# First attention of a four-layer kernel: three hand-written issue orders changed on TensorE, ScalarE and VectorE

## What is computed

```
ln_out = _ln(hidden_states, ln_w, ln_b)
q  = _ln(_fp8_linear_pertensor(ln_out, wq, ...))      # 16 heads of 128
k  = _ln(_fp8_linear_pertensor(ln_out, wk, ...))      # 8 groups, two heads share one
v  =     _fp8_linear_pertensor(ln_out, wv, ...)
core = _gqa(q, k, v)                                  # softmax(q k / sqrt(128)) v
qx = _ln(_fp8_linear_pertensor(ln_out, wqx, ...))
kx, vx = split(einsum(cond, w_kv_x)); kx = _ln(kx)
xout = _gqa(qx, kx, vx)
catq = _div_clamp_fp8(concatenate([core, xout]), proj_smooth)
out  = einsum(catq, wproj) * (proj_in_scale * proj_w_scale)
```

## Time and profile before

| what | value |
|---|---|
| median of 3 runs | 1542.64 us (1542.45 to 1543.8) |
| span of the profiled execution, first to last instruction | 1540.9 us |
| mean granted TensorE clock of the core | 0.985 |
| busy shares over the span | PE 94%, DVE 58%, ACT 49%, POOL 34% |
| the first attention in the trace | about 22 to 470 us |
| query copies (L753) / key copies (L758) | 64 / 32 |
| mean of one query copy, one key copy | 797 ns, 780 ns |

### The profile page before, as it was taken

One profiled execution on the slowest core, in us unless ns is written; L12 is line 12 of the kernel. 1 busy time (PEld: TensorE's weight loads), 2 busy tenths in 40 slices (PEclk: granted clock), 3 DMA queues, 4 the chain that ended last, 5 costly groups with the idle time before them and its releaser, 6 DMA issues. The chain is left out here.

```text
span 1540.9 us, 22220 instructions
## 1 busy us (share of the span) xinstructions
PE 1443.8 (94%) x6908; PEld 1036.8 (67%) x6910; DVE 895.8 (58%) x1940; ACT 762.5 (49%) x2116; POOL 528.4 (34%) x519
## 2 busy tenths in 40 slices
PE   4999998899999999999999999999968999999998
PEld 1677777777874555557787979776745666665656
DVE  7888988888875242323555454554686555553322
ACT  4888888888882211110343535343456555544210
POOL 2667677877761000000542424221111333321000
PEclk9999999999999999999999999999979999999999
DMA  5211000200007311112100000002141000001120
GB/s 198 80 41 59 8 5 1 94 1 1 1 1 291 144 57 48 54 49 76 66 1 1 1 0 9 20 1 83 37 181 45 1 1 1 1 29 34 51 64 21
DMA packets 21304, 71.65 MB, mean 47 GB/s; under 512 B 3859, under 2 KB 6291, under 8 KB 18245
## 3 DMA queue, kind: packets, MB, share of 16 engines
q1 hardware_dynamic: 12980, 57.37, 10.0%
q10 hardware_dynamic: 8208, 12.87, 2.6%
HBM read 69.01 MB, written 1.22 MB: 46 GB/s over the span
## 5 line engine op out<-in xcount | busy, mean ns | idle before, releaser
L1190 ACT ACTIVATE l0f_silu<-bank 128x512 f32<-128x512 f32 x48 | 28.6, 597 | 199.9 <-PE bank L1114 189.8
L828 POOL TENSOR_TENSOR l0a_stepped<-l0a_y,l0a_m 128x512 f32<-128x512 bf16 x64 | 74.0, 1156 | 94.4 <-DVE l0a_m L575 93.0
L1293 DVE TENSOR_TENSOR l0f_product<-l0f_silu,bank 128x512 f32<-128x512 f32 x48 | 32.9, 688 | 123.8 <-ACT l0f_silu L1190 123.7
L856 POOL TENSOR_TENSOR l0a_head_rstd<-l0a_head_var,all_minus_half 128x4 f32<-128x4 f32 x96 | 100.8, 1054 | 7.6 <-DVE l0a_head_var L597 7.6
L427 PEld LDWEIGHTS bank<-l0a_k_t,l0a_q_t 128*128 128x128 f32 x512 | 63.2, 191 | 49.1 <-ACT l0a_q_t L753 45.1
L767 ACT ACTIVATE l0a_work<-bank,l0a_neg_max 128x128 f32<-128x128 f32 x256 | 90.2, 370 | 0.9 <-DVE l0a_neg_max L610 0.9
L1126 PEld LDWEIGHTS bank<-all_weights_a,l0f_hidden 128*128 128x128 f32 x384 | 72.9, 190 | 25.2 <-issue 17.0
L1730 DVE TENSOR_TENSOR all_weights_a<-bank,all_cols 128x512 f32<-128x512 f32 x64 | 43.9, 690 | 77.9 <-PE bank L1559 45.9
L1126 PE MATMUL bank<-all_weights_a,l0f_hidden 128*128 128x256 f32 x384 | 88.9, 379 | 0.0
L427 PE MATMUL bank<-l0a_k_t,l0a_q_t 128*128 128x128 f32 x512 | 72.1, 284 | 17.1 <-ACT l0a_q_t L753 16.7
L2608 POOL TENSOR_TENSOR l3a_q_scale<-l3a_q_var,all_minus_half 128x4 f32<-128x4 f32 x32 | 32.4, 1013 | 159.7 <-DVE l3a_q_var L2398 159.7
(11 more groups left out here) (434 smaller groups left out, 3825.8 us busy)
## 6 DMA issues: line engine op xcount, KB each, us to landing
l0f_spread<-l0f_weights ACTq DMA_DIRECT2D x32, 192.0 KB, 2.7
all_weights_a<-in_l_w_q SPq DMA_DIRECT2D x2, 2048.0 KB, 14.5
l0f_spread<-l0f_weights ACTq DMA_DIRECT2D x32, 128.0 KB, 2.9
all_weights_b<-in_l_e_gate_up SPq DMA_DIRECT2D x1, 3200.0 KB, 10.6
all_weights_b<-in_l_e_gate SPq DMA_DIRECT2D x1, 3072.0 KB, 10.2
all_weights_a<-in_l_e_up SPq DMA_DIRECT2D x4, 768.0 KB, 7.2
all_weights_a<-in_l_e_down SPq DMA_DIRECT2D x1, 3072.0 KB, 16.8
l3a_spread<-l3f_weights SPq DMA_DIRECT2D x10, 256.0 KB, 3.5
```

The source lines that it names most:

```text
L828: done = g.tensor_tensor(stepped[:, 0:n], value, step, ALU.add)
L856: g.tensor_tensor(head_rstd[:, m % 2, :], head_var[:, m % 2, :], res.minus_half[:, 0:HU], ALU.pow)\
```

## The change

Three lists of `march` in `layer0_attention` are reordered. No instruction is added, removed or altered, and no wait is.

```
 PE:
-                               in_tile(F_TILE, first_up, F_UP), (project_out, later(at_query, 11)),
-                               (turn, later(at_norm, 3)), (project, range(STEPS))])
+                               in_tile(F_TILE, first_up, F_UP), (turn, later(at_norm, 3)),
+                               (project_out, later(at_query, 11)), (project, range(STEPS))])
 DVE:
-            march(VTS, STEPS, [(variance, later(at_norm, 1)), (row_inverse, later(at_query, 5)),
-                               (row_max, later(at_query, 4)), (normalise, later(at_norm, 2)),
+            march(VTS, STEPS, [(variance, later(at_norm, 1)), (row_max, later(at_query, 4)),
+                               (normalise, later(at_norm, 2)), (row_inverse, later(at_query, 5)),
 ACT:
-            march(VTS, STEPS, [(exponentials, later(at_query, 5)), (scale_probs, later(at_query, 6)),
-
-                               (keep_values, later(at_plain, 1)), (keep_turned, later(at_norm, 3)),
+            march(VTS, STEPS, [(keep_turned, later(at_norm, 3)), (exponentials, later(at_query, 5)),
+                               (scale_probs, later(at_query, 6)), (keep_values, later(at_plain, 1)),
                                (prepare, range(STEPS)), (keep_probs, later(at_query, 7)), (square, at_norm),
```

## The result

The changed kernel takes 1590.53 us (median of 4 runs, 1587.45 to 1592.28) against 1542.55 us before in the same runs. The ratio is 1.0309, 95% interval 1.0295 to 1.0323: slower by 3.1%, some 48 us. Forecast were 1592 us, in a range of 1573 to 1611.

What follows compares the result with a forecast made beforehand. PE was taken to bound the cross half outright and to share the bound in the core half. Terms 40 + 6 + 4 = 50 us on a span of 1540.9, plus 1.7, gave about 1592 us, range 1573 to 1611.

Steps and rivals of the forecast that it cites:

- The deciding term: Odd steps: key copies ahead of scaling on ACT delay PE's turn_probs by 1.28 us, 31 times, 40 us.
- up to 6 us may come back: Tiles 8 and 9: a longer tile lets late DVE and POOL catch up, returning up to 6 us.
- The even steps: Query copy ahead of exponentials: scores need both, starting 2.19 to 2.22 us after the copy, so order wins nothing.
- the late copy of step 6: Core tiles, step 6: the query copy comes 0.31 us later than the exponentials started before.
- The ring in core tiles: Steps 6 and 0: copy, exponentials, DVE, turn take 6.52 us against 6.29; two pairs in 8 tiles, 4 us.
- The six places at 1.0 us: Tiles 4 to 7: PE's earlier turn waits for normalised rows where DVE has extra work, 6 us.
- DVE's list: Steps 2 and 4: normalise fills the time until the later exponentials end, costed at nothing.
- the PE waits: Rival: PE's 16.7 us of waits before the scores disappear, giving 1526 us; chance 4%.
- a draw: Rival: even steps tie and key scaling is somehow covered, giving 1543 us; chance 3%.
- only queries move: Rival: lists do not bring key copies ahead of scaling, so 6 + 4 remain, 1553 us; chance 5%.
- a bound by DVE: Rival: slow rounding closes the ring or late normalising pushes the next, 1612 us or above; chance 8%.
- cross tiles of 28.6 us: Sign of being right: a cross tile lasts some 28.6 us in place of 26.

Runs made afterwards that it cites:

- e1: Changed kernel with key copies back behind scale_probs and keep_values on ACT, query copies still ahead of the exponentials: 1557.20 us, ratio 1.0098.
- e2: Kernel before with key copies alone moved ahead of scale_probs on ACT: 1574.40 us, ratio 1.0207.
- e9: Changed kernel with PE turning keys right behind the scores, ahead of mix, ACT's list untouched: 1567.91 us, ratio 1.0163.
- e3: Kernel before with PE's list alone as in the change, turn ahead of project_out: 1543.46 us, ratio 1.0009.
- e5: Kernel of e1 with quantise, quantise_early and centre_queries put ahead of row_inverse on DVE: 1553.92 us, ratio 1.0073.
- e6: Changed kernel with DVE's old list, reciprocals ahead of row maximum and normalising: 1591.63 us, ratio 1.0320.
- e7: Kernel before with DVE's new list alone, row maximum and normalising ahead of reciprocals: 1542.98 us, ratio 1.0001.

## Why the prediction was right, and where its terms were not

**The deciding term.** Key copies ahead of `scale_probs` were predicted to hold `turn_probs` by 1.28 us, 31 times, 40 us. The mechanism is shown by e1, e2 and e9. The hold measured is 1.25 to 1.27 us in each place, and the size in all is 33.3 us (e1 against the changed kernel). The count was one too high: the first scaling starts at 50.22 us, behind the key copies of both step 3 and step 5 of tile 0 (34.26 and 43.61), so 30 holds are left. In cross tiles 1 to 7 the difference of the two kernels is 2.54 us a tile, where two times 1.28 is 2.56. In core tiles 10 to 13 it is 2.40. The term was too large at its edges: tile 8 gives 0.1 back, tile 9 takes 1.4, and tiles 0 and 15, with one hold each, take 0.0 and 1.2. The prediction had put "up to 6 us may come back" in tiles 8 and 9 into the lower end, not into the sum; 3.8 came back there.

**The even steps.** The score needs copy and exponentials, whatever their order: right. Where PE waits before scores in the changed kernel, in 38 places, exponentials end the wait, never the query copy, and e1 gained nothing. Only three of the 38 lie before 259 us: in nearly all of the cross half PE comes to the scores too late to wait. But the sum is not equal. From copy to scores it takes 2.32 us and not 2.19 to 2.22; the row below the reciprocal shows PE starting 1.64 after the first exponential (373.57 to 375.21), where DVE starts 1.52 after it. This 0.1 us comes four times a tile. Together with the late copy of step 6 (0.31, as predicted) it makes the 0.67 us by which e1's core tiles are longer (26.12 against 25.45): the four pairs are longer by 0.44, 0.08, 0.08 and 0.07.

**The ring in core tiles.** "Copy, exponentials, DVE 3.64, turn: 6.52" was the wrong reason, and that the term came out near its size is luck: 4 us stood in the sum, and in e1 core tiles 10 to 13 are 2.7 us longer by the release and the late copy just told, and tile 14 is 2.1 longer for a reason not settled. The pair of steps 6 and 0 takes 6.35 after the change. From the reciprocal to the end of `normalise` it is 2.57 us now (375.09 to 377.66), not 3.64, and PE does not wait for the rows (`turn_probs` 377.96, turn 0.44 later). I had carried over a stretch that held a slow rounding instruction.

**The six places at 1.0 us.** This step failed in its reasoning: e3 has the earlier turn and loses 0.8 us, within noise. A DVE that is late by a constant is waited for once. It is waited for again and again only when its lateness comes round: in the company of ACT's new order the reciprocal depends on exponentials that depend on the turned query. e1 is 1.01 us a tile longer than before in tiles 1 to 7, 7.1 in all, of which the slower release, four times 0.08 a tile, is 2.2 us at most; e5 takes about 3 us out of the ring. In the changed kernel PE does wait for rows in tiles 5 to 7, twice in each, 0.41 to 1.68 us, where about 1 us was named; but it also waits in tiles 2 to 4, for 3.6 us in five places, where the prediction had the rows in time. Parts of the 7.1 us, and 2.1 us in tile 14 of e1, are not settled.

**DVE's list.** Costed at nothing; e6 and e7 agree.

**The sum.** 40 + 6 + 4 stood against 33.3 + 14.6. Errors of 7 too much and 5 too little met in a total that is 2 off; that it is so close is luck. The rivals: the PE waits did not go, they rose from 16.7 to 24.3 us; a draw, "only queries move" as a reading of the code, and a bound by DVE did not come about. The time that "only queries move" was given, 1553, was measured in e1 as 1557. The page Perfetto Trace Analysis of the Trainium skill (section Optimization Strategy) asks for what a gap waits on to start sooner; e3 did this for the turn and e1 for the copy, and neither shortened the time (1543.46 and 1557.20 us against 1542.67): in e3 the copy still stood behind the exponentials on ACT, and in e1 the scores waited for the exponentials, now behind the copy.

**What was named as a sign:** 50 us of waits before key copies (54.9 came), some 30 waits before `turn_probs` of over 1 us (30, longest 1.1), cross tiles of 28.6 us (30.35 came, of which the kernel before already had 26.80 and not 26), core tiles of 28.3 (28.52), a cross window with PE under 37 of 40 us (35.32).

## What to carry to other kernels

When a list of work is reordered for one kind of item, look at every kind that the same entry handles, and at what then waits in front of it: here the queries were meant and the keys cost two thirds of the loss. Moving one of two conditions of a wait forward gains nothing when the other takes its place on the same in-order engine. A late producer costs its lateness once; it costs it each time only if its start depends on the consumer, so look for the ring before multiplying.

## What the runs showed of the hardware

A rounding instruction of 256 elements on DVE takes 0.23 us or over 1 us, by what POOL does. In the kernel before, steps 6 and 7 of tile 12:

```profile
365.81 1.16 POOL L832 TENSOR_TENSOR l0a_cat<-l0a_stepped,l0a_m 128x512 fp32r<-128x512 f32 x1 [0.16 <-issue]
365.83 1.22 DVE L571 TENSOR_SCALAR l0a_e<-l0a_yq 128x256 uint16<-128x256 uint16 x1
```

It starts 0.02 after a POOL product of 1.16 us and ends with it. In the changed kernel the same instruction of the same step, here of tile 11, meets an idle POOL, whose next product comes 0.7 later:

```profile
375.67 0.23 DVE L571 TENSOR_SCALAR l0a_e<-l0a_yq 128x256 uint16<-128x256 uint16 x1
...
376.37 0.67 POOL L827 TENSOR_TENSOR l0a_stepped<-l0a_yq,l0a_mq 128x256 f32<-128x256 bf16 x1 [1.28 <-DVE l0a_mq L575]
```

It takes 0.23 us. The Trainium skill, page SBUF — State Buffer, section Who interferes with whom, says that a DVE `tensor_scalar` may use a second pair of ports which it shares with GpSimd, and that whoever comes second waits for the whole instruction of the first; these rows agree with it. So does the whole trace of the kernel before: of its 96 rounding instructions of 256 elements (L569, L571, L575) 29 took over 0.8 us, and each of these started while a rounding product of POOL was under way and ended within 0.15 us of its end; of the 49 that started outside one, none took over 0.3. An order that delays DVE by 0.66 us can so save it 1.0.

The release of PE by ACT's last exponential came 0.12 us later than that of DVE by the same event (375.21 and 375.09). No run here tells whether this lies in the semaphore or in PE's way from a wait to its first matmul.
